# The first layer's output projection over all 128 rows of its operands, zero beyond the 17 that hold data

## The reference, cut to what matters

```python
h = tok(x) ; h = concat([h, txt])                    # 32 x 69 x 256
# layer 0
Z = softmax(causal(Q K^T / 4)) V                     # per head, 69 x 16
h = h + einsum('bhsd,de->bse', Z, WO) + 16 * bO      # WO: 16 x 256
h = h + gate * expert_ffn(layernorm(h))              # one of 8 experts per token
# layer 1
h = h + attention(layernorm(h)) @ Wproj + bproj      # Wproj: 256 x 256
h = h + quantized_conv_ffn(layernorm(h))
```

## Time and profile before

| | |
|---|---|
| median of 3 runs | 924.82 us (922.55 to 928.59) |
| profiled execution | 923.76 us, its span 921.9 us |
| granted TensorE clock, mean over the span | 0.926 |
| busy share of the span | PE 86%, PEld 76%, DVE 65%, ACT 48%, POOL 41% |
| projection of layer 0 (L1500) | 64 matmul records, 16 places |

### The profile page before, as it was taken

How to read it: one execution, slowest core, us unless ns; L and a number is a source line. 1 busy time by engine, 2 the same in 40 slices (tenths; PEclk the granted TensorE clock), 3 DMA queues, 4 the chain that set the end, 5 groups by cost and what they waited for, 6 DMA issues and landing times.

```text
span 921.9 us, 20693 instructions
## 1 busy us (share of the span) xinstructions
PE 795.2 (86%) x7145; PEld 697.2 (76%) x7145; DVE 600.6 (65%) x1444; ACT 439.0 (48%) x1048; POOL 382.2 (41%) x514
## 2 busy tenths in 40 slices
PE   2899999999999999249999299999999999999633
PEld 2788888998898888126676289898888888888532
DVE  0256665666666654452222035889999999999893
ACT  0244444344444442212222156767778777876552
POOL 0224444444444432222221376646665666543100
PEclk9999999999999996569999699989999999999755
DMA  5316630100000022112212100000000000000000
GB/s 159 90 53 208 184 85 17 19 11 8 8 8 10 11 78 75 41 27 67 70 54 57 28 10 14 8 7 14 19 15 14 15 14 15 18 10 8 9 11 12
DMA packets 23981, 36.41 MB, mean 39 GB/s; under 512 B 10037, under 2 KB 21210, under 8 KB 23114
## 3 DMA queue, kind: packets, MB, share of 16 engines
q1 hardware_dynamic: 14474, 26.20, 10.1%
q0 software_dynamic: 5808, 5.63, 2.8%
q10 hardware_dynamic: 3600, 3.28, 1.1%
HBM read 27.21 MB, written 7.88 MB: 38 GB/s over the span
## 4 chain that ended last, share of the span: by engine, by line
PE 42%; DVE 31%; issue 13%; DMA 7%; ACT 4%; POOL 2%; SPq 1%; DVEq 0%; ACTq 0%; POOLq 0%
PE bank_h L1431 4%; PE bank_c L1468 4%; DMA h<-in_txt 4%; PE bank_b L1459 3%; PE bank_e L1586 3%; PE bank_c L1602 2%; DVE stats L899 2%; PE bank_f L1586 2%; PE bank_d L1602 2%; DVE diff L1107 2%; DVE w L1164 2%; PE bank_b L1500 2%; DVE w L1133 2%; DVE rowmax L1099 2%; DVE w L1139 2%
## 5 line engine op out<-in xcount | busy, mean ns | idle before, releaser
L454 POOL TENSOR_TENSOR qbd<-qt,consts_f 128x560 f32<-128x560 f32 x128 | 163.1, 1280 | 199.5 <-PE bank_e L1403 75.7
L462 POOL TENSOR_TENSOR veps<-mv,consts_f 69x2 f32<-69x2 f32 x64 | 12.4, 194 | 148.7 <-DVE mv L903 110.8
L581 ACT ACTIVATE pt<-bank_g 69x448 f32<-69x448 f32 x64 | 34.9, 546 | 76.6 <-PE bank_h L1413 76.6
L1468 PE MATMUL bank_c<-patches,w_tok 128*128 128x74 f32 x384 | 52.4, 292 | 13.8 <-DMA br<-in_br 13.8
L576 ACT ACTIVATE prob<-diff 112x345 f32<-112x345 f32 x64 | 31.4, 491 | 65.5 <-DVE diff L893 65.5
L1468 PEld LDWEIGHTS bank_c<-patches,w_tok 128*128 128x128 f32 x384 | 50.2, 209 | 13.8 <-issue 13.8
L732 ACT ACTIVATE w<-w,conv 128x138 f32<-128x138 f32 x128 | 54.8, 492 | 10.4 <-DVE w L1116 10.4
L500 POOL DMA_INDIRECT diff<-expert_rows,tile_tokens x25 | 25.5, 1018 | 80.1 <-PE bank_a L1578 59.0
L1777 PE MATMUL bank_b<-f,w 128*69 128x256 bf16 x256 | 37.4, 309 | 15.4 <-ACT w L745 14.5
L481 POOL DMA_INDIRECT expert_lists<-token_no,slot_i x32 | 38.5, 1203 | 21.6 <-issue 14.3
L1431 PE MATMUL bank_h<-values,pt 69*69 69x68 f32 x512 | 39.4, 233 | 8.7 <-ACT pt L581 6.8
(11 more groups left out here) (237 smaller groups left out, 2349.3 us busy)
## 6 DMA issues: line engine op xcount, KB each, us to landing
w<-in_w SPq DMA_DIRECT2D x2, 4096.0 KB, 16.0
patches<-in_patches SPq DMA_DIRECT2D x16, 222.0 KB, 2.6
expert_results<-prob ACTq DMA_DIRECT2D x25, 128.0 KB, 1.9
expert_rows<-x SPq DMA_DIRECT2D x16, 138.0 KB
out<-h SPq DMA_DIRECT2D x16, 138.0 KB
f_raw<-in_f SPq DMA_DIRECT2D x2, 1024.0 KB, 8.1
patches<-in_b SPq DMA_DIRECT2D x1, 2048.0 KB, 10.3
wqkv<-in_wqkv SPq DMA_DIRECT2D x2, 768.0 KB
```

Source lines behind the costliest of these rows:

```text
L454: pool.tensor_tensor(qbd[u % 2][:], q.broadcast_to([128, NG, HPB, QG]), head_mask.unsqueeze(1).unsqueeze(3).broadcast_to([128, NG, HPB, QG ...
L1468: ins = mm(banks["c"][:, m * 2 * IMG:(m + 1) * 2 * IMG], w_tok[:, c, m * 128:(m + 1) * 128], patch_v[:, bass.ds(s, 1), c, :].rearrange("p ...
```

## The change

The two operands of the projection are taken over all 128 rows. For this `wo0` has 128 rows in place of 17 (the same place and length in each partition), and GpSimd clears it and the 128 rows of `ot[:, 0]` at the start, behind the four clears there; ScalarE still writes rows 0 to 16 of `ot`, and the loads rows 0 to 16 of `wo0`. Every wait for the clears counts two more, and SP waits for the six of them before it loads `wo0`. No instruction changes its place in an engine's list.

```diff
-        wo0 = sb("wo0", [DH + 1, D])
+        wo0 = sb("wo0", [128, D])
...
+            sp.wait_ge(clears_done, 6)
             sp.dma_start(wo0[0:DH, :], a["wo0"]).then_inc(attn0_w_in, 16)
             sp.dma_start(wo0[DH:DH + 1, :], a["bo0"].unsqueeze(0)).then_inc(attn0_w_in, 16)
...
             nc.gpsimd.memset(seen[:, :], 0.0).then_inc(clears_done, 1)
+            nc.gpsimd.memset(ot[:, 0, :, :], 0.0).then_inc(clears_done, 1)
+            nc.gpsimd.memset(wo0[:], 0.0).then_inc(clears_done, 1)
...
-            act.wait_ge(clears_done, 4)
+            act.wait_ge(clears_done, 6)
...
-            dve.wait_ge(clears_done, 4)
+            dve.wait_ge(clears_done, 6)
...
-            pe.wait_ge(clears_done, 4)
+            pe.wait_ge(clears_done, 6)
...
-                        ins = mm(banks["b"][0:T, b * D:(b + 1) * D], ot[0:DH + 1, 0, b, 0:T], wo0[:], start=True, stop=True)
+                        ins = mm(banks["b"][0:T, b * D:(b + 1) * D], ot[:, 0, b, 0:T], wo0[:], start=True, stop=True)
...
-            pe.wait_ge(clears_done, 5)
+            pe.wait_ge(clears_done, 7)
```

## The result

The changed kernel takes 916.44 us in the median of 6 runs (914.91 to 917.55), the kernel before 925.22 of 6 (922.55 to 929.4). The ratio is 0.990 with a 95% interval of 0.987 to 0.993. The forecast was 922.6 us in a range of 918.6 to 928.0, so the gain is 8.8 us where 2.2 were expected, and the time lies under the range.

A forecast was written before the change was run, and what follows sets the result against it. TensorE nearly bounds the first layer, DVE the second. Fourteen projections at 0.14 us (1.96) plus 0.2 at the fifteenth make 2.2 us: 921.6 against the profiled 923.76, 922.6 us against the median; range 918.6 to 928.0.

The forecast's parts named there:

- The edges and their size: First-layer projections: entry to fourth matmul 0.91 to 0.77 us, exit 0.30 to 0.216; entry saves 14 x 0.14 = 1.96 us.
- The exit gain: Behind the projection's fourth matmul: 0.085 us saved, counted as nothing in steps where VectorE's work covers it.
- L1431's wait: PE's wait for ScalarE's copy after the projection: would grow from 0.49 to about 0.58 us, taking up the exit's saving.
- The copy to `ot` in step 18: Sixteenth projection, at 371.66 us: its load must wait for the copy ending at 371.61, so it saves nothing.
- The clears and SP's wait: Kernel start: two more clears, 0.4 us, ready by about 1.9; zero cost, SP's wait itself under 0.1 us.
- The fifteenth, at 350.59, ... entry and exit count, 0.2 us: Fifteenth projection: PE is on the chain before and behind it, so both savings count, 0.2 us.
- a hazard in layer 1: Second layer: one half-clock stretch more or less, 4.0 us each; chance 0.09 of more, 0.07 of less.
- the clock goes the right way: Second layer: the existing half-clock stretch is missing, 4.0 us less, giving 918.6 us; chance 0.07 for less half clock.
- the 3 us by which the runs of before themselves lie off their middle one: Whole kernel: run spread of 3 us put into the range around the forecast and two rivals.
- The rival of loads that stop overlapping: First-layer projections: with 128 rows the three inner loads become exposed, 3.6 us more, giving 928.4 us; chance 0.02.
- The rule that rows cost a load nothing: Projection weight loads: a skill page says columns matter, not the contraction; by that alone the sum would be zero.

The follow-up runs named there:

- e1: Changed kernel with 128 rows only in the projections of steps 3 to 15 and 17 rows in the last three; 921.16 us, ratio 0.999 to the kernel before.
- e2: Changed kernel with 17 rows in the projections of steps 3 to 15 and 128 rows in the last three; 917.81 us, ratio 0.992 to the kernel before.
- e8: The changed kernel run once more, unaltered, on the same chip as the 96-row version; 916.18 us, ratio 0.989 to the kernel before.
- e5: Changed kernel with 128 rows in step 17's projection alone and 17 rows in the other 15; 918.86 us, ratio 0.993 to the kernel before.
- e12: Changed kernel plus unused 74-column matmuls in the pauses of steps 16 to 18 and 30 more ahead of the expert stage; 920.39 us, ratio 0.996.
- e15: Changed kernel plus unused 256-column matmuls in the pauses of steps 16 to 18 and 20 more ahead of the expert stage; 918.14 us, ratio 0.994.

## Why the prediction was wrong, step by step

- **The edges and their size were right.** Entry 0.11 us and first to fourth 0.65, sum 0.76 (I took 0.77); exit 0.216 (as taken). The term was 14 x 0.14 = 1.96 us; the fourteen steps from the first projection to the fifteenth shrank by 2.2 us in the profiled pair, 0.15 in most and 0.29 in the first.
- **The exit gain is covered, as said, but at another wait.** I looked for it at L1431's wait and named that as the test of the step. That wait did not move. L1444's did, by 0.115 us: PE meets the work behind the projection there first.
- **The copy to `ot` in step 18** does set the sixteenth projection's start: 0.04 us lie between the end of the copy and the projection after the change as before.
- **The clears and SP's wait cost nothing that can be told from the spread of the start.** The two clears took 0.21 and 0.32 us and ended at 1.86; SP issued `wo0` at 6.25 (6.09 before).
- **The step that failed is "The fifteenth, at 350.59, ... entry and exit count, 0.2 us".** From the fifteenth projection to the sixteenth the pair shows 4.7 us, since the granted clock behind that projection was taken as given and fell 7.6 us later (8.4 us behind its start, not 0.8); e1 against e2 shows that the last three projections do this. I had counted its entry and exit and priced the clock only as a hazard in layer 1, with a chance on either side, where a fall of the clock stood right behind one of the very instructions that the change touches: in the earlier trace rows the stretch from 351 us is at 0.51, and the fifteenth projection is at 350.5. The rival "the clock goes the right way" had the right sign and the wrong place.
- **The spread was misread too.** The runs' 922.55 to 928.59 us went into the range as "the 3 us by which the runs of before themselves lie off their middle one". The 64 runs at 925 us or more have the lower clock: their mean granted clock has medians of 0.920 to 0.923 in the five sets, the others' 0.926 to 0.929. The change takes such runs away (none in 24), which is a part of the 8.8 us that the profiled pair does not hold. With 128 rows in the last three projections none of eight is left (e2), with 17 there four of ten (e1). That in these runs the clock falls in step 16 is inferred: no profile of the kernel before is of one. The profiles of e1 and e5, with 17 rows in step 16, have such a fall; the 14 with 65 or more rows there and no added 17-row matmul have none.
- **Some of the steps' gain is given back by the clock.** In ten of the fifteen profiles of kernels without edges in the steps before step 16 (the changed kernel's repeats among them), and in none of the five with edges, the clock is at half for 3.4 us near 240 us. The windows from the ninth to the tenth projection in e8, and then in the first profile of the same kernel:

```profile
229.00:250.00 21.00, 19.92 (x199) 18.38 (x197) 13.30 (x38) 7.81 (x21) 8.94 (x14) 0.92 0.06 9
```

```profile
229.00:250.00 21.00, 19.92 (x210) 18.57 (x209) 13.55 (x38) 8.77 (x24) 9.30 (x14) 1.00 0.06 9
```

  From the first to the thirteenth projection it is 248.4 us in e8, against 246.7 and 248.6 of the kernel before. So in such runs the 1.9 us are almost lost, and most of what the change brings comes from the later fall. Why it falls there was not tried.
- **The rival of loads that stop overlapping did not come**: the load of L1503 starts 0.06 us ahead of its matmul and under the embedding's. The Trainium skill, TensorE: Matmul & The Clock Gate, section "The mechanism" of Part 3, says of loads under running matmuls "only when row_grp differs" (a sentence ahead of it allows a background weight buffer as well); the trace disagrees with the "only" in both kernels, 0.05 us from matmul to the next load where both take more than 64 rows, 0.20 where only one does.
- **The rule that rows cost a load nothing** (the Trainium skill, TensorE: Matmul & The Clock Gate, section "LDWEIGHTS (loading the stationary operand)") nearly holds for the load, with medians of 136 ns at 17 rows and 141 at 128, and not for the kernel.

Open: how the edges and the row count share the effect on the clock, and what differs between two runs of one kernel that puts them in different places of the spread. With edges and 128 rows three of ten runs are at or under 919.5 us, without edges and with 65 rows eight of twenty, without edges and with 96 or 128 rows all 31. Each was compared with the kernel before on its own chip, and 65 rows never beside 128 in one set.

## What to carry to other kernels

Before a term is priced at tenths of a microsecond, look whether the granted clock changes within a few microseconds of it; a small group of instructions next to a pause can decide at which clock the next 20 us run. A wide spread of single runs, on one of these chips in two heaps at 920 to 925 and 926 to 930 us, went with different granted clocks here, and it deserves a case of its own in the range. Where a matmul of 17 or 64 rows stood in a stream of larger ones, zeros up to 65 rows or more took its edges away, 0.15 us ahead and inside and 0.09 behind, for 5 ns more a record; all 128 rows were the safer choice for the clock in this kernel.

## What the runs showed of the hardware that I had not expected

- Matmuls of 17 and 64 rows between matmuls of 69 to 128 rows don't have their first load hidden (0.205 us from start to start, 0.70 from first to fourth, 0.304 behind), those of 65, 96 and 128 do (0.112 us, 0.65, 0.216). A column count of 17 between larger ones (L1490) has no such edge: 0.098 us ahead and 0.06 behind.
- With all rows from the 18th on zero, and every instruction at the same place and of the same length within 3 ns, 12 of 20 runs with 65 rows are above 919.5 us and none of 31 with 96 or 128, in different sets.
- TensorE was busy back to back for 12.8 us at 1.2 GHz in e12, with sixty records against 74 columns, and the clock stayed there; in e15, with records against 256 columns, it rose to 2.4 GHz 5.9 us after their start. One profile each; what made the difference was not tried apart.
